# Graph network kernel: GpSimd's gather program written out with indices read in place, matrix stores in runs of 2.5 KB, and a reordered exit of layer 1

## The reference

```
x = layernorm(x + gat2(x))        # two attention layers, 4 heads: tanh in the first
x = layernorm(x + gcn3(x))        # three convolutions with edge weights, then h @ Wf
x = layernorm(x + sum_of_sources(x))
x = layernorm(x + egnn2(x))       # two convolutions with edge features, batch norms
```

```
e = leaky_relu(el[src] + er[dst], 0.2)
ex = exp(e - segment_max(e, dst)[dst])
out = segment_sum(z[src] * ex / segment_sum(ex, dst)[dst], dst) + b
```

## Time and profile before

| | |
|---|---|
| median of 3 runs | 6481.95 us |
| the profiled execution | 6478.01 us, its span 6476.2 us |
| TensorE / VectorE / ScalarE / GpSimd busy | 68% / 58% / 33% / 55% of the span |
| preparation, up to GpSimd's last start | 0 to 173 us |
| layer 0 | to some 2320 us |
| layer 1 | to some 4584 us |
| exit of layer 1 | to some 4651 us |
| convolutions | to 6476 us |

### The profile page before, as it was taken

How to read it: one execution, slowest core, us unless ns; L and a number is a source line. 1 busy time by engine, 2 the same in 40 slices (tenths; PEclk the granted TensorE clock), 3 DMA queues, 4 the chain that set the end, 5 groups by cost and what they waited for, 6 DMA issues and landing times.

```text
span 6476.2 us, 121634 instructions
## 1 busy us (share of the span) xinstructions
PE 4376.9 (68%) x31749; PEld 2994.7 (46%) x31749; DVE 3741.5 (58%) x10803; ACT 2158.1 (33%) x6178; POOL 3540.2 (55%) x4137
## 2 busy tenths in 40 slices
PE   1677766776777655555555565565688888888775
PEld 1344443444444333333333333333577666776664
DVE  4787777777777756666666666666411112224445
ACT  0555555555555533434333343343200000000000
POOL 4788878887878858888888888888000000000000
PEclk9777777777777766666666666666699999999998
DMA  6555555555565545555555555555599898999876
GB/s 100 155 173 168 167 172 160 165 164 174 162 173 170 159 120 138 144 143 137 146 145 143 134 143 146 133 146 147 216 414 406 331 415 330 414 402 404 363 311 266
DMA packets 847601, 1376.36 MB, mean 213 GB/s; under 512 B 413399, under 2 KB 596584, under 8 KB 831277
## 3 DMA queue, kind: packets, MB, share of 16 engines
q1 hardware_dynamic: 562451, 863.04, 37.8%
q0 software_dynamic: 128976, 222.12, 14.6%
q10 hardware_dynamic: 156040, 289.55, 12.8%
HBM read 1000.91 MB, written 373.27 MB: 212 GB/s over the span
## 4 chain that ended last, share of the span: by engine, by line
POOL 21%; issue 19%; DMA 18%; DVE 14%; PE 13%; SPq 4%; DVEq 3%; ACT 3%; POOLq 2%; ACTq 1%
POOL arena L844 19%; DMA arena<-adj_w_d 8%; DMA arena<-adj_c_d 5%; PE bank L1907 3%; PE bank L1908 3%; PE bank L1911 3%; DMA arena<-msg_d 3%; SPq L524 2%; ACT arena L2043 2%; DMA arena<-table_d,arena 2%; POOL arena L826 2%; DVE arena L1228 1%; DVE arena L1103 1%; DVE arena L1096 1%; SPq L761 1%
## 5 line engine op out<-in xcount | busy, mean ns | idle before, releaser
L844 POOL DMA_INDIRECT arena<-table_d,arena x3136 | 3233.2, 1031 | 932.6 <-issue 768.5
L1744 PE MATMUL bank<-arena 128*128 128x500 f16 x3750 | 1299.3, 501 | 1374.0 <-DVE arena L1159 1199.8
L1744 PEld LDWEIGHTS bank<-arena 128*128 128x128 f16 x3750 | 429.5, 123 | 2050.8 <-issue 1786.0
L2043 ACT ACTIVATE arena<-arena 128x128 f16<-128x128 f16 x3750 | 1121.3, 393 | 98.7 <-DVE arena L1078 95.2
L1907 PE MATMUL bank<-arena 125*128 125x250 f16 x3750 | 870.8, 277 | 170.1 <-DMA arena<-adj_w_d 126.3
L1908 PE MATMUL bank<-arena 125*128 125x250 f16 x3750 | 867.0, 276 | 0.0
L2135 ACT ACTIVATE arena<-arena 128x600 f32<-128x600 f32 x250 | 175.8, 703 | 1955.2 <-DVEq L1230 1945.2
L1765 PE MATMUL bank<-arena 128*65 128x40 f32 x7500 | 691.6, 271 | 137.2 <-ACT arena L2092 115.4
L1765 PEld LDWEIGHTS bank<-arena 128*65 128x65 f32 x7500 | 658.8, 186 | 173.5 <-ACT arena L2135 143.5
L1746 PE MATMUL bank<-arena 128*128 128x500 f16 x1875 | 645.8, 463 | 0.0
L1076 DVE TENSOR_SCALAR arena<-arena 128x500 f16<-128x500 f16 x1875 | 585.7, 367 | 44.3 <-issue 29.0
(11 more groups left out here) (263 smaller groups left out, 4155.3 us busy)
## 6 DMA issues: line engine op xcount, KB each, us to landing
arena<-adj_w_d SPq DMA_DIRECT2D x720, 625.0 KB, 10.6
arena<-adj_c_d SPq DMA_DIRECT2D x345, 625.0 KB, 11.4
adj_w_d<-arena ACTq DMA_DIRECT2D x125, 1250.0 KB
arena<-msg_d SPq DMA_DIRECT2D x1250, 103.5 KB
msg_d<-arena POOLq DMA_DIRECT2D x196, 552.0 KB
adj_c_d<-arena ACTq DMA_DIRECT2D x125, 625.0 KB
arena<-table_d,arena POOLq DMA_INDIRECT x3136
arena<-in_edge_features ACTq DMA_DIRECT2D x625, 51.0 KB
```

The lines of the kernel that those rows point to most:

```text
L844: g_.indirect_dma_start(ring[:, i, k * XC:(k + 1) * XC], None, table_d[layer], bass.IndirectOffsetOnAxis(ap=idx_cur[:, i, k:k + 1], axis=0 ...
L1744: mm(wb, lhsT=row_oh[:, slot, c, i, :], rhs=col_oh[:, slot, c, :], start=(c == 0 and i == 0), stop=(c == CH - 1 and i == 1))
L2043: last = act_(row_oh[:, slot, c, i, :], row_oh[:, slot, c, 2, :], ACT.Copy, scale=rec[:, c * REC + 2 + i:c * REC + 3 + i])
```

## The change

GpSimd's blocks are no longer run in loops: all 98 of each layer are written out, the gather reads its index column straight from `row_idx`, and `idx_cur`, the copies and their semaphore are gone. The waits for pace, gathers and stores stay where they were. Each group's counts are stored by two DMAs and its weights by four, 2,500 bytes for each partition each; DRAM layout and bytes stay. At the exit, TensorE first makes all degrees by 50 products of one column, ScalarE alone evacuates the block products, with the first two square roots put behind its fifth block and the first half's low features behind its twentieth, TensorE's top-scale products stand before its thirteenth, and VectorE takes the first half's layer norm ahead of the degrees.

```diff
-            def copy_indices(j, i, k):
-                g_.tensor_copy(idx_cur[:, i, k:k + IDX], row_idx[:, bass.ds(j * BK + k, IDX)]).then_inc(s("idx_here"), 1)
...
+            def block(j):
+                i = j % RING
+                if j >= RING or layer:
+                    place = pool.value_load(pace_row[0:1, layer, j:j + 1], ...)
                 for k in range(BK):
-                    if place is not None and k % 2 == 0:
+                    if (j >= RING or layer) and k % 2 == 0:
                         wait_reg(pool, s("dve_step"), place + k * PER_BLOCK // BK)
-                    if k % IDX == IDX - AHEAD_IDX:
...
-                    if k % IDX == 0:
-                        wait_reg(pool, s("idx_here"), ...)
                     g_.indirect_dma_start(ring[:, i, k * XC:(k + 1) * XC], None, table_d[layer], bass.IndirectOffsetOnAxis(
-                        ap=idx_cur[:, i, k:k + 1], axis=0)).then_inc(gathered[i], 16)
+                        ap=row_idx[:, j * BK + k:j * BK + k + 1], axis=0)).then_inc(gathered[i], 16)
...
-            for it in (rounds(pool, NBLK // RING) if layer else range_from_one(pool, NBLK // RING)):
-                for i in range(RING):
-                    block(it * RING + i, i, it + uses_before[i], ...)
+            for j in range(NBLK):
+                if layer == 0 and j == RING:
+                    pool.wait_ge(s("items_back"), 32)
+                block(j)
@@ stores
-            return b * 32 + 32 * sum(...)
+            return b * STORES + STORES * sum(...)          # CUTS = 1, STORES = 16 * 6 * CUTS
...
+                per = TH // CUTS
+                for t in range(0, T, per):
+                    act.dma_start(adj_c_d[bass.ds(group, 1), :, t:t + per, :]..., flat(stage_c[:, slot, t:t + per, :])).then_inc(adj_stored[slot], 16)
                 act.wait_ge(s("adj_evacuated"), windows_before(layer, b, n + 1))
+                for h in range(2):
+                    for l in range(2):
+                        for t in range(0, TH, per):
+                            act.dma_start(adj_w_d[bass.ds(group, 1), :, h, l, t:t + per, :]..., flat(stage_w[:, slot, h, l, t:t + per, :])).then_inc(adj_stored[slot], 16)
@@ exit: VectorE
-            per_node_vector(d)
-            degrees_vector(d)
-            top_scale(d, 0)
+            d.wait_ge(s("agg_stored"), 16 * B * 2)
             for h in halves(0):
                 t = half(h)
                 layer_norm(d, t)
+                if h == halves(0)[0]:
+                    degrees_vector(d)          # from the psum bank of the degrees, behind deg_psum
+                    top_scale(d, 0)
@@ exit: TensorE, per_node_tensor
+            for t in range(T):
+                last = mm(degrees[:, t:t + 1], lhsT=seg_t[:, t * NT:(t + 1) * NT], rhs=we[:, 0:1], start=True, stop=True)
+            last.then_inc(s("deg_psum"), 1)
             for b in range(B):
+                if b == TOP_AFTER:             # 12
+                    top_scale_tensor(pe, 0)
                 if b >= 4:
-                    pe.wait_ge(s("pn_evac_act" if b % 2 else "pn_evac"), (b - 4) // 2 + 1)
+                    pe.wait_ge(s("pn_evac"), b - 3)
...
+            pe.wait_ge(s("pn_evac"), B)
@@ exit: ScalarE, per_node_scalar
-            for b in range(1, B, 2):
+            for b in range(B):
+                if b == STD_AFTER:             # 5
+                    std_scalar(act, half(halves(0)[0]))
+                    std_scalar(act, slice(0, T))
+                if b == LOW_AFTER:             # 20
+                    low_features(act, 0, 0)
                 act.wait_ge(s("pn_psum"), b + 1)
```

More of the change, by code:

```diff
@@ L594, in pair @@
             return ((bank[0], bank[1]), (bank[2], bank[3]), (bank[5], bank[7]))[n % 3]
+        STD_AFTER = 5
+        TOP_AFTER = 12
+        LOW_AFTER = 20
         def pn_sum(b):
@@ L625, in wait_some @@
                 eng.wait_ge(semaphore, value)
+        CUTS = 1
+        STORES = 16 * 6 * CUTS
         def stage_stores(layer, b, slot):
-            return b * 32 + 32 * sum(B for l in range(layer) if slot < len(ADJ[l]))
+            return b * STORES + STORES * sum(B for l in range(layer) if slot < len(ADJ[l]))
         LOADS = 16 * WG
@@ L828, in block, with store @@
[L828 to L832, removed]
+            def store(j):
+                i, uses = j % RING, j // RING + uses_before[j % RING]
+                pool.wait_ge(gathered[i], (uses + 1) * (16 * BK))
+                g_.dma_start(msg_d[j * BLK:(j + 1) * BLK, :].rearrange("(p k) f -> p (k f)", k=BK), ring[:, i]).then_inc(msg_stored[i], 16)
@@ L844, in block @@
-                    g_.indirect_dma_start(ring[:, i, k * XC:(k + 1) * XC], None, table_d[layer], bass.IndirectOffsetOnAxis(
-                        ap=idx_cur[:, i, k:k + 1], axis=0)).then_inc(gathered[i], 16)
-                    if former is not None and k == BK // 8:
-                        store(j - 1, (i - 1) % RING, former)
-                    if former is not None and k == BK // 2:
-                        ready((i - 1) % RING, former)
-            def former_uses(it, i):
-                return it + uses_before[(i - 1) % RING] - (1 if i == 0 else 0)
@@ L859, in blocks_pool @@
                     pool.wait_ge(s("redo_stored"), 16 * B)
-            if layer == 0:
-                for i in range(RING):
-                    block(i, i, 0, None if i == 0 else 0)
-                pool.wait_ge(s("items_back"), 32)
-            for it in (rounds(pool, NBLK // RING) if layer else range_from_one(pool, NBLK // RING)):
-                for i in range(RING):
-                    block(it * RING + i, i, it + uses_before[i], None if first(it) and i == 0 else former_uses(it, i))
-            it = NBLK // RING
-            for i in range(NBLK % RING):
-                block(it * RING + i, i, it + uses_before[i], former_uses(it, i), last=i + 1 == NBLK % RING)
-            last = NBLK - 1
-            store(last, last % RING, last // RING + uses_before[last % RING])
-            ready(last % RING, last // RING + uses_before[last % RING])
+            for j in range(NBLK):
+                if layer == 0 and j == RING:
+                    pool.wait_ge(s("items_back"), 32)
+                block(j)
+            store(NBLK - 1)
+            ready(NBLK - 1)
         @block.gpsimd
@@ L1362, in redo_vector @@
                         d.drain().then_inc(s("redo_made"), 1)
-        def per_node_vector(d):
-            for b in range(0, B, 2):
-                d.wait_ge(s("pn_psum"), b + 1)
-                v.tensor_copy(per_node[:, 2 * b:2 * b + 2, :], pn_sum(b)).then_inc(s("pn_evac"), 1)
         ln_count = [0]
@@ L2207, in identity_conv_scalar, with low_features @@
             std_block(act, B - 1, n)
+        def low_features(act, n, at_):
+            act.wait_ge(s("x_hl"), 2 * n + at_ + 1)
+            t = half(halves(n)[at_])
+            act_(x_two[:, t, :], x_one[:, t, :], ACT.Copy, scale=1.0 / LOW).then_inc(s("x_low"), 1)
         def conv_scalar(act, n):
```

50 lines of the change are left out of this document (21 added, 29 removed).

## The result

The changed kernel takes 6339.68 us (median of 4, 6336.28 to 6342.01) against 6479.77 us for the kernel before, measured together with it (median of 4, 6473.11 to 6491.6): ratio 0.9777, interval 0.9766 to 0.9788, 140 us or 2.2% faster. I had forecast 6401 us in 6350 to 6440.

What follows compares the result with a forecast made beforehand. GpSimd, working back to back in both layers, was taken to bound the kernel. Copies -80, fetches +3, store waits -3, exit -1 sum to -81 us: 6397 from the profiled execution, 6401 against the median; range 6350 to 6440.

Steps and rivals of the forecast that it cites:

- the copies: Both layers: removing the index copies, 770 of which count, from GpSimd gains 80 us, between 69 and 105.
- the store waits: GpSimd's wait for its gathers before a message store: shorter rows and fewer copies gain 3 us, between 0 and 10.
- the fetches: GpSimd's straight-line code, now fetched as it goes, costs 3 us, between 0 and 27.
- the exit: Exit of layer 1: VectorE's wait moves from block products to the root; gain 1 us, bounds 0 and 21.
- What bounds the layers: Both layers: GpSimd works back to back to each layer's end, so what its round costs less, the layers lose.
- Rival 1: More goes: copies 105 us, store waits 10, exit 21; 136 us less, 6346 us. Chance 0.12.
- Rival 4: Layers: fetching straight-line code stalls GpSimd's gathers; at 1 us a block 6591 us, slower. Chance 0.06.
- ScalarE's issues: Matrix stores: 500 more issues, 1.44 us more a group on ScalarE, hidden by its waits for VectorE; uncovered, 180 us.
- Rivals 2 and 3: 2: VectorE limits layer 0, only layer 1 gains, 6440 us, chance 0.10. 3: pace waits absorb everything, 6480 us, chance 0.04.

Runs made afterwards that it cites:

- the later message store: Changed kernel with the old coarse matrix stores, message store and its `ready` issued two gathers later: 6339.84 us, ratio 0.9779 to the kernel before.
- GpSimd's part: Kernel before with GpSimd's blocks written out, indices read in place, no copies; stores and exit as before: 6386.03 us (0.9852); other chips 7898.96 us (1.0196).

## Why the prediction was wrong in size

In the prediction's own terms: the copies gave 125 us for 80, the store waits 4 us net for 3, the fetches cost nothing for 3, the exit gave 1 for 1, and some 7 us (ahead of the layers, between them and behind them) had no term. Together 137 us for 81.

- **What bounds the layers: right** for the chips it was made on. GpSimd worked back to back in both traces, and what a gather costs less, the layers lost (125 us by the groups, 129 us in the stretches).
- **The copies: the step that failed.** I bounded the term by 69 us (quiet) and 105 us (loaded means) and took 80, "If it is VectorE's fixed work in each group, most of what hit a copy will hit the next gather instead". It measured 125 us, 0.162 us for a copy. That assumption is what failed: the gathers that are left did not get longer by what had struck the copies. The loaded means were not too high but too low: they let the other gathers keep their length, which made 1.325 and 1.323 us a gather, and 1.322 and 1.313 came. In layer 1 the mean gather fell from 1030 to 1008 ns. Of these 22 ns some 13 are the one in four behind a copy (1071 ns, against 1017 for those with nothing before them; I had reckoned 30 ns more for it, not 54), the other 9 came off all the rest. So 103 us stand at the copies, near my upper bound, and some 20 us more have a cause that is not shown. Rival 1 had the upper end with a chance of 0.12 and 6346 us; its other two causes (store waits 10, exit 21) did not come, so it was near in number but wrong in two of three steps. The rule of the Trainium skill (GPSIMD Engine Reference, Key points) that GpSimd contends with VectorE for SBUF was given as speaking for the lower end. No run here separates that contention, and the measured term lies above the upper end, so the inference from the rule failed, not the rule.
- **The message store: a wait that I costed without its neighbour.** I wrote "Between 0 and 10 us; I take 3, since two copies fewer in front of a store also bring GpSimd there sooner". This is the right mechanism with both sizes wrong. Alone, the fine stores gave 17 us. Without them the faster GpSimd meets its own landing gathers for 52.8 us instead of 11.4 (180 to 4450 us). In the whole change the two cancel: 10.4 us of this wait stand there after. That the term came out near my 3 us is luck. Had the stores not been cut, the kernel would be at 6378 us.
- **The straight-line program: right that it costs next to nothing.** Its idle "issue" is 979.4 us in 2960 pieces; without the two long ones (50.4 us between the layers, 27.25 us at items_back) that is 0.305 us each. Rival 4 did not come. That GpSimd fetched while it ran shows in the queue of instructions, 115 packets instead of 65. Whether leaving the loop also gave something is not shown.
- **ScalarE's issues: hidden, as said**, on these chips, though they made 333.9 us of new waits. On the other kind the finer stores cost 118 us alone (7870.81 against 7752.97) and some 117 us on top of the rest (8016.34 against 7899.37, with an exit 5 us shorter): whether the issues or the shorter rows cost that was not separated. On the first kind the later message store reaches the same time, 6339.84 us, with two issues a group, and leaves VectorE 434.3 us of waits for rows instead of 317.9: the finer stores spent cover that the later store keeps.
- **The exit: right.** Forecast 1 us, VectorE standing 18 us for the root, degrees 21.9 us. The trace has 1.1 us, 17.75 us, and these rows of TensorE and ScalarE, the root 27.4 us behind the first degree product:

```profile
4451.61 21.16 PE L1873 MATMUL bank<-arena 34*125 34x1 f32 x100 [5.75 <-DVEq L1382]
```

```profile
4477.72 1.28 ACT L2178 ACT_TABLE_LOAD   x1
4479.01 0.23 ACT L2178 ACTIVATE arena<-arena 125x25 f32<-125x25 f32 x1
```

- **Rivals 2 and 3** fell: both layers gave their part, and GpSimd's waits for VectorE's queue stayed at the 0.3 us that every gather has (12.8 us for L1216, in 42 pieces).

## What to carry to other kernels

When an instruction is taken out of the engine that sets the pace, price it by the loaded means of that stage and not by the quiet ones: here the loaded means gave 105 us, the quiet ones 69, and 125 came, and what had lengthened the copies did not lengthen the gathers that were left. And a faster engine shortens the grace that its own transfers had: list each wait of that engine on a landing, with the time between issue and wait, and ask what the tail of the landings does when that time shrinks. Such a wait can be taken away at its place, by two gathers more of grace, as well as at its cause, by shorter rows in the stores that stand ahead in the DMA queues.

## What was not expected of the hardware

One store of 1250 KB in rows of 10,000 bytes, issued by another engine, held the landing of gathers back enough to stop GpSimd for up to 3.8 us at 6 to 10 us after its issue; the same bytes in rows of 2,500 left 10.4 us of such waits from 180 to 4450 us instead of 52.8. The 50 degree products of one column took 21.16 us, as long as those of 8 columns (21.13 us) and nearly as those of 129 (21.86 us). The granted clock was 0.50 for the first and the last of these and 1.00 for those of 8 columns, so in these rows the time is the same at either level. And one and the same kernel took 6482 us on some chips and 7741 to 7779 us on others, with pauses of TensorE of 0.5 to 3.3 us between products that wait for nothing in the trace. A change measured on one chip is measured for one kind of chip: this one is 2.2% faster on one, and GpSimd's part and the finer stores, each alone, were 2.0% and 1.5% slower on the other.
